# The order of work in layer 1's attention: the next block's input and its projections placed earlier, one projection to a slot

## The reference

```
tp = _swiglu(time_emb @ w_t1 + b_t1) @ w_t2 + b_t2
shift1, scale1, shift2, scale2 = split(tp, 4)
h = _rmsnorm(x, g1) * (1 + scale1) + shift1
q, k, v = split(h @ w_qkv + b_qkv, 3)
q = _rope(q); k = _rope(k)       # o0 = x0*cos - x1*sin ; o1 = x1*cos + x0*sin
attn = softmax(q @ k.T / sqrt(16))
x = x + (attn @ v) @ w_ao + b_ao
h = _rmsnorm(x, g2) * (1 + scale2) + shift2
x = x + _swiglu(h @ w_fc + b_fc) @ w_fo + b_fo
```

## Time and profile before

| | before |
|---|---|
| median of three runs | 2191.68 us |
| the profiled execution | 2191.38 us, of which 2189.6 us are the span of the trace |
| PE busy | 2021.7 us, 92% |
| DVE, ACT, POOL busy | 59%, 47%, 20% |
| layer 1's attention | from 363.40 us (first scores) to 709.83 us (first matmul of the MLP that needs its output) |

### The profile page before, as it was taken

How to read it: one execution, slowest core, us unless ns; L and a number is a source line. 1 busy time by engine, 2 the same in 40 slices (tenths; PEclk the granted TensorE clock), 3 DMA queues, 4 the chain that set the end, 5 groups by cost and what they waited for, 6 DMA issues and landing times.

```text
span 2189.6 us, 44527 instructions
## 1 busy us (share of the span) xinstructions
PE 2021.7 (92%) x15460; PEld 1655.9 (76%) x15460; DVE 1283.0 (59%) x2473; ACT 1021.9 (47%) x1645; POOL 443.5 (20%) x413
## 2 busy tenths in 40 slices
PE   7989998778777999999998999999999999999998
PEld 6877886656666888887777777777788787787887
DVE  5846664555556656564455554455766777776664
ACT  3534555454544333334444444444545555554444
POOL 4622103343332101011111111111210212220000
PEclk9999999889999999999999999999999999999999
DMA  6000001011000000000000000000000000000000
GB/s 221 21 9 8 11 7 34 28 36 42 28 26 29 11 20 19 10 15 6 7 6 6 1 5 7 5 3 2 15 7 5 11 10 10 5 5 1 29 19 29
DMA packets 23543, 42.06 MB, mean 19 GB/s; under 512 B 2322, under 2 KB 13074, under 8 KB 22930
## 3 DMA queue, kind: packets, MB, share of 16 engines
q1 hardware_dynamic: 23442, 40.65, 5.6%
HBM read 28.06 MB, written 4.19 MB: 15 GB/s over the span
## 4 chain that ended last, share of the span: by engine, by line
PE 72%; issue 11%; DVE 9%; POOL 4%; ACT 2%; DMA 0%; DVEq 0%; POOLq 0%; ACTq 0%; SPq 0%
PE psum L608 19%; PE psum L610 18%; PE psum L609 18%; PE psum L703 2%; PE psum L716 2%; PE psum L650 2%; PE psum L801 2%; PE psum L749 2%; PE psum L735 1%; PE psum L692 1%; DVE xn L1120 1%; PE psum L543 1%; POOL k L1340 1%; DVE h_lo L1141 1%; DVE pb L1190 1%
## 5 line engine op out<-in xcount | busy, mean ns | idle before, releaser
L608 PE MATMUL psum<-h_hi,w_lo 128*128 128x512 f32 x1056 | 437.0, 414 | 14.1 <-DVE h_lo L1141 8.5
L610 PE MATMUL psum<-h_hi,w_hi 128*128 128x512 f32 x1056 | 415.7, 394 | 0.0
L609 PE MATMUL psum<-h_lo,w_hi 128*128 128x512 f32 x1056 | 415.5, 393 | 0.0
L1242 DVE TENSOR_TENSOR hid_lo<-hid,hid_hi 128x512 fp32r<-128x512 f32 x256 | 193.6, 757 | 261.1 <-ACT hid_hi L994 261.1
L994 ACT ACTIVATE hid_hi<-hid 128x512 fp32r<-128x512 f32 x256 | 161.8, 632 | 219.2 <-PE psum L610 132.1
L1187 DVE TENSOR_REDUCE mx<-psum 128x8 f32<-128x512 f32 x192 | 132.4, 690 | 204.2 <-PE psum L692 116.5
L608 PEld LDWEIGHTS psum<-h_hi,w_lo 128*128 128x128 f32 x1056 | 201.7, 191 | 61.7 <-issue 13.3
L1324 POOL TENSOR_TENSOR rstd<-ms,half_t 128x4 f32<-128x4 f32 x64 | 65.2, 1019 | 903.1 <-DVE ms L1115 480.3
L610 PEld LDWEIGHTS psum<-h_hi,w_hi 128*128 128x128 f32 x1056 | 200.2, 190 | 44.4
L609 PEld LDWEIGHTS psum<-h_lo,w_hi 128*128 128x128 f32 x1056 | 201.9, 191 | 35.3
L989 ACT ACTIVATE hid<-psum,vec 128x512 f32<-128x512 f32 x192 | 131.9, 687 | 176.4 <-PE psum L610 163.3
(11 more groups left out here) (144 smaller groups left out, 3669.9 us busy)
## 6 DMA issues: line engine op xcount, KB each, us to landing
swapped<-rows SPq DMA_DIRECT2D x64, 128.0 KB, 2.0
stage<-in_w_dram SPq DMA_DIRECT2D x24, 256.0 KB, 2.7
stage<-in_w_dram SPq DMA_DIRECT2D x8, 512.0 KB, 3.5
out_dram<-xres SPq DMA_DIRECT2D x8, 512.0 KB, 2.9
xres<-in_x_dram SPq DMA_DIRECT2D x1, 3584.0 KB, 18.6
modw_mod<-in_modw_dram SPq DMA_DIRECT2D x2, 1536.0 KB, 13.6
stage<-in_w_dram SPq DMA_DIRECT2D x8, 384.0 KB, 3.2
stage<-in_w_dram SPq DMA_DIRECT2D x8, 192.0 KB, 2.4
```

The lines of the kernel that those rows point to most:

```text
L608: nc.tensor.matmul(dst, s_lo, m_hi, start=start and j == 0, stop=False)
L609: nc.tensor.matmul(dst, s_hi, m_lo, start=False, stop=False)
L610: ins = nc.tensor.matmul(dst, s_hi, m_hi, start=False, stop=stop and j == len(pairs) - 1)
L1242: nc.vector.tensor_tensor(hid_lo[:, slot, :], hid32[:, slot, :], hid_hi[:, slot, :].bitcast(F32), ALU.subtract).then_inc(sem["hid"], 1)
```

## The change

Only the list of layer 1's attention is written in another order. `stats` to `split` of the next block stand one to two slots earlier (`split` in slot 3, before in slot 4). The four projections of the next block stood as two in slot 5 and, a block later, two in slot 0; now there is one in each of the slots 4 to 7. The exchange by DMA comes with the projection, the rotation one slot later, the expansion one more. Part 1 of the next block is thus projected before the block begins. `share` and `load` move from slot 0 to slot 1. The shift onto ACT, DVE, POOL and SP follows from the list. Two lines of each side:

```diff
-        return [own("scores", 0), prev("probs_t", 7), own("k", 1), prev("pv", 6), own("q", 1), own("k_swap", 1),
-                own("q_swap", 1), own("share"), nxt("load"),
+        return [own("scores", 0), prev("probs_t", 7), prev("pv", 6), own("k_out", 1), own("q_rot", 1), nxt("stats"),
...
-                own("scores", 5), own("probs_t", 4), own("pv", 3), nxt("k", 0), nxt("q", 0), nxt("k_swap", 0),
-                nxt("q_swap", 0),
+                own("scores", 6), own("probs_t", 5), nxt("k_out", 0), nxt("q_rot", 0), nxt("k", 1), nxt("k_swap", 1), own("pv", 4),
```

More of the change, by code:

```diff
@@ L102, in order_of @@
     if layer == 1:
-        return [own("scores", 0), prev("probs_t", 7), own("k", 1), prev("pv", 6), own("q", 1), own("k_swap", 1),
-                own("q_swap", 1), own("share"), nxt("load"),
[L105 to L109, removed]
-                own("scores", 5), own("probs_t", 4), own("pv", 3), nxt("k", 0), nxt("q", 0), nxt("k_swap", 0),
-                nxt("q_swap", 0),
-                own("scores", 6), own("probs_t", 5), own("pv", 4), nxt("k_rot", 0), nxt("q_rot", 0),
-                own("scores", 7), own("pv", 5), own("probs_t", 6), nxt("k_out", 0), nxt("q_out", 0)]
+        return [own("scores", 0), prev("probs_t", 7), prev("pv", 6), own("k_out", 1), own("q_rot", 1), nxt("stats"),
+                own("scores", 1), own("probs_t", 0), own("v", 0), prev("pv", 7), own("v_out", 0), own("v", 1), own("v_out", 1),
+                nxt("norm"), own("share"), nxt("load"),
+                own("scores", 2), own("probs_t", 1), prev("merge"), own("q_out", 1), nxt("turn"), own("pv", 0),
+                own("scores", 3), own("probs_t", 2), prev("proj"), own("pv", 1), nxt("split"),
+                own("scores", 4), own("probs_t", 3), nxt("k", 0), nxt("k_swap", 0), prev("back"), own("pv", 2),
+                own("scores", 5), own("probs_t", 4), nxt("k_rot", 0), nxt("q", 0), nxt("q_swap", 0), own("pv", 3),
+                own("scores", 6), own("probs_t", 5), nxt("k_out", 0), nxt("q_rot", 0), nxt("k", 1), nxt("k_swap", 1), own("pv", 4),
+                own("scores", 7), own("probs_t", 6), nxt("q_out", 0), nxt("k_rot", 1), nxt("q", 1), nxt("q_swap", 1),
+                own("pv", 5)]
     if layer == 3:
```

## The result

The changed kernel takes 2127.57 us in the median of four runs (2124.38 to 2128.70), the kernel before beside it 2192.44 us. The ratio is 0.9703, with a 95% interval of 0.9686 to 0.9720: 3.0% faster. Forecast were 2126 us. The profiled execution took 2127.41 us, its span 2125.6 us, 64.0 less than before. On another chip, later, the same kernel took 2127.42 us, ratio 0.9705 (0.9691 to 0.9718). One execution of one experiment, e6_q1_in_slot0, took 8045.59 us where its three others took 2115.73 to 2117.29; it has no profile and is left out of every reading here.

A forecast was written before the change was run, and what follows sets the result against it. Bound: layer 1's chain from projection to scores. Period 35.0 for 44.5 saves 57.1 us, block 0 5.0, last block 7.5: 69.6, less 4 for the clock, taken as 65 off 2191.4, gives 2126 us; range 2108 to 2157.

The forecast's parts named there:

- The bound: Layer 1's attention: the dependence chain from projection to scores, 12.1 us, sets the period of 44.5 us; no engine is full.
- Step 1 and 2: Rotation of k, then ACT's kx, rows of k 1 and qb: next scores 0 start 14.0 us after projection k 0.
- Step 3: DVE takes cosine of q 1, division after pv 5, then scores 0, and is through with them at 18.1 us.
- Step 4: From PE's transposes through projections and copies of v to ACT's xn: second copy at 22.4, xn ends at 25.3 us.
- rival A: Half the gain: a chain behind three new queue heads closes 4 to 5 us late; period 39.5, 2153 us, chance 0.20.
- Steps 5 to 7: From xn's end through merge, output projection, y and split: 28.7, 31.6, 33.0, 34.9; next k 0 starts at 35.0 us.
- The list of PE's gaps: PE's waits in a new block: 4.8 us in five pieces of 0.5 to 1.5, beside about 30.2 us of work.
- Block 0 and the last block: Gains at the ends of layer 1's attention: 5.0 us in block 0, 7.5 us in the last block.
- The clock, 4 us taken off for it: Half clock after PE's new short gaps in layer 1: 0.6 us in each of 6 blocks and at the ends.
- rival B: PE at half clock for output projection and scores in each block: 22 to 29 us lost, 2147 us, chance 0.08.
- Nothing that DVE's small operations lose to POOL: DVE's variance operations beside POOL's rotation of q 1: contention costs 0 to 0.3 us a block, taken as 0.
- Rivals C and D: C: DVE over a slot behind PE in slots 4 to 7, 2216 us, 0.05; D: period set elsewhere, about 2191, 0.05.

The follow-up runs named there:

- e6_q1_in_slot0: List of e4_norm_split with the projection of q 1 moved from slot 7 into slot 0 of its own block, its rotation into slot 1: 2117.14 us.
- e1: Changed kernel, but part 1 of k and q projected in its own block, in slot 0, as before the change: 2153.71 us.
- d0: Changed kernel with one more reduction on DVE ahead of that of scores 0 in each layer 1 block: period 36.1 us, total 2118.55 us.
- d2: Changed kernel with the same additional DVE reduction ahead of scores 2 instead of scores 0: period 35.5 us, total 2116.40 us.
- e7: Changed kernel with only the split put ahead of the output projection's bias, norm left in place: period 34.0 us, total 2117.57 us.
- e3: Changed kernel with pv 5 put before the projection of q 1 in slot 7: period 35.7 us, total 2124.52 us.
- e2: Changed kernel, but k and q of a part projected together, part 0 in slot 4, part 1 in slot 6: 2148.89 us.
- c1: Kernel before the change, with six matmuls of constants filling PE's wait for qb ahead of scores 0, first block excepted: 2195.62 us, ratio 1.0045.
- e4_norm_split: Changed kernel with norm between the two copies of v and split before the output projection's bias: period 33.8 us, total 2112.22 us.

## Why the prediction was right, step by step

- *The bound* (latency from projection to qb, not PE's work): right. e1 puts part 1 back behind the start of its block and loses 26 us.
- *Step 1 and 2, scores 0 at 14.0*: 13.8. The gap for qb was to be under 1 us: 0.25.
- *Step 3, DVE is the link at scores 0*: right to 0.1 us, and d0 and d2 show the place. One sentence of mine contradicted it: "some 1.5 us after PE issued them" for the start of DVE's scores 0; by the same steps it was 2.6, and it is 2.8 (503.93 to 506.76).
- *Step 4, xn ends at 25.3*: 25.8. ACT waits 0.38 us before xn, where the step has no wait, and the second copy of v starts 0.1 us later than forecast. That is the 0.5 us by which the period, 35.5, exceeds the 35.0, and with it 3 of the 57.1 us. The room for kx of part 1 was 0.5 by my count; in the trace ACT idles 0.20 us before the first copy of v and 0.40 before the second. No more than this stood against rival A at this place, and it did not come.
- *Steps 5 to 7*: right, each within 0.1 us of its length. e7 confirms y before h_hi as the link.
- *The list of PE's gaps*: partly wrong. I missed the wait of pv 6 for the division (1.18); it takes the place of the 1.1 before the transposes of slot 1, and e3 shows that it is the same slack at another place. The 0.8 before scores 0 is 0.25 and the 0.5 before the output projection is nothing. Together the waits are 4.0 us for 4.8 in a longer period, since PE's work was taken too small: it is 31.5 us a block (188.96 by 6) and not the 30.2 that I took from layer 3. The period did not hang on this term, but the floor of 30.2 for "PE alone" was too low.
- *Block 0 and the last block*: 5.0 and 8.1 for 5.0 and 7.5.
- *The clock, 4 us taken off for it*: mis-sized and at the wrong place. In the six blocks and the last one the clock is 1.00 and nothing is lost; rival B is out. Block 0 has 0.90, for 0.85 before. "All MLPs keep their lengths to 1 us" did not hold in the profiled execution: layer 2's MLP loses 2.9 us in its first block.
- *The total*, 2126 for 2127.57, is closer than its parts, and so much is luck: 3.3 us too many in the six blocks and 3.0 in layer 2's MLP, less 0.6 in the last block, were about covered by the 4 that were taken off for half clock in layer 1, of which there was none. (69.6 less 4 is 65.6; I wrote 65.) The range has a slip too: a period of 34 would have given 2118 to 2120 us, with 6 to 8 blocks, and not 2112.
- *Nothing that DVE's small operations lose to POOL*: they took 0.16 us each. They ran from 510.42 on, when POOL's last sum was over (508.81 and 1.29), so the 0 held, but the contention itself was not put to the test.
- *Rivals C and D*: out for this list. e2 shows how near C is: with two cosines in one slot DVE stands 3.75 us and PE 2.2.

## What to carry to other kernels

Where every engine takes its queue in order, follow one period through all queues by hand with the durations of the old trace, and include what stands in front on each engine; it gave the period to 0.5 us of 35. The same work costs nothing in a slot in which PE waits anyway and its full length in one in which it doesn't, so spread operations that hold a queue one to a slot (e2), and put what the next stage waits for (h_hi) before what only a later one needs (y). When an entry is moved, ask in each queue what it will stand in front of at its new place: e6 freed one chain and held up another. Waits in pieces of up to 1.5 us left TensorE's clock at full in every block of the loop; behind one of 5 us it fell in each. In PE's busy time that is 18.8 of the 53.8 us, but c1 shows only 1.8 us a block for the longest gap, and no gain in the total.

## What the runs showed of the hardware that was not expected

The same gap doesn't always cost the same. At the start of layer 2's MLP PE waits for the first block's input, in the trace before and in that after (the transposes' rows, and the stretch of before):

```profile
1544.35 1.10 PE L650 MATMUL psum<-vec,xn 128*128 128x128 f32 x8 [2.97 <-DVE xn L1122]
```

```profile
1530.29:1562.58 32.29, 29.32 (x137) 23.89 (x136) 23.05 (x41) 20.85 (x25) 8.49 (x7) 1.00 0.06 21
```

```profile
1478.09 1.97 PE L649 MATMUL psum<-vec,xn 128*128 128x128 f32 x8 [2.95 <-DVE xn L1121]
```

A wait of 2.97 was followed by full clock and a block of 32.29 us, one of 2.95 by half clock and 35.15 us (clock 0.90). Over all traces that block took 32.3, 33.6 to 33.9 or 35.1 to 35.2 us. The runs don't show this to be an effect of the changed list: e4_norm_split took 33.9 us there in one trace and 32.3 in the other, with the same program. So 3 us of a profiled total can come and go with the clock at one gap, which is why the periods are read first.

In the loop of layer 2's attention a block takes 63.9 us or, in none to two of its turns in each trace, about 70 to 71. In the changed kernel's trace:

```profile
1145.66:1209.59 63.93, 61.50 (x754) 49.35 (x753) 32.96 (x62) 29.72 (x50) 11.17 (x11) 1.00 0.02 5
1209.59:1280.96 71.37, 64.44 (x754) 51.54 (x753) 32.97 (x62) 29.60 (x50) 11.16 (x11) 0.95 0.02 5
```

```profile
1256.77 0.69 PE L691 MATMUL psum<-k_sb,q_sb 64*64 64x64 f32 x32 [2.49 <-issue]
...
1259.66 1.13 PE L748 MATMUL psum<-pt,v_sb 64*64 64x64 f32 x31 [2.03 <-issue]
```

PE stands there for 2.49 and 2.03 us with nothing to wait for that the profile shows, while packets of the instruction queue arrive, and the clock falls behind it. The traces of before and after have two such turns each, so they don't move the comparison of the two. The profiled execution of e7_split_only had none and took 2103.93 us; its five others, which have no profile, took 2116.75 to 2119.07. That instruction loading causes these turns was not tested.
